# W_down and W_up laid out with neighbouring rows in a partition, in a persistent adapter kernel

## The reference

```
h = einsum('bsh,bhk->bsk', x, W_down[role]) + b_down[role]      # 1024 -> 512
h = gelu(h)                                                     # exact gelu
u = einsum('bsk,bkh->bsh', h, W_up[role]) + b_up[role]          # 512 -> 1024
y = x + u
out = layernorm(y) * gamma[role] + beta[role]
```

## Time and profile before

| | us |
|---|---|
| median of 3 runs | 1418.1 (1417.81 to 1418.21) |
| the profiled execution, its time | 1418.03 |
| its span | 1416.3 |
| TensorE busy in the span | 1401.5 |
| VectorE busy | 1207.1 |
| ScalarE busy | 778.0 |
| GpSimd busy | 200.9 |

### The profile page before, as it was taken

One profiled execution on the slowest core, in us unless ns is written; L12 is line 12 of the kernel. 1 busy time (PEld: TensorE's weight loads), 2 busy tenths in 40 slices (PEclk: granted clock), 3 DMA queues, 4 the chain that ended last, 5 costly groups with the idle time before them and its releaser, 6 DMA issues.

```text
span 1416.3 us, 29328 instructions
## 1 busy us (share of the span) xinstructions
PE 1401.5 (99%) x6175; PEld 1158.7 (82%) x6176; DVE 1207.1 (85%) x1456; ACT 778.0 (55%) x2053; POOL 200.9 (14%) x300
## 2 busy tenths in 40 slices
PE   8999999999999999999999999999999999999997
PEld 6888888888888888888888888888888888888886
DVE  7799988888888888888888899988888888888887
ACT  5555555555555555555555555555555555555555
POOL 3377311100000000000000377311100000000000
PEclk9999999999999999999999999999999999999999
DMA  9678777766666656666666778767766666666664
GB/s 228 184 227 236 210 218 199 212 195 200 184 194 198 194 183 196 198 193 185 194 199 192 215 227 230 225 199 211 207 197 185 200 199 186 185 195 201 189 186 149
DMA packets 208868, 283.49 MB, mean 200 GB/s; under 512 B 25791, under 2 KB 155584, under 8 KB 208846
## 3 DMA queue, kind: packets, MB, share of 16 engines
q1 hardware_dynamic: 201870, 269.60, 62.3%
q0 software_dynamic: 5888, 12.07, 5.0%
q10 hardware_dynamic: 1088, 1.57, 0.4%
HBM read 183.27 MB, written 99.88 MB: 200 GB/s over the span
## 4 chain that ended last, share of the span: by engine, by line
PE 97%; DVE 1%; DMA 1%; ACT 0%; issue 0%; DVEq 0%; ACTq 0%
PE p_down L1077 16%; PE p_up L1079 16%; PE p_down L1079 16%; PE p_up L1077 16%; PE p_down L1078 16%; PE p_up L1078 16%; DMA row<-in_L_cond_W_down 0%; DMA x_quad<-in_x 0%; DVE row L997 0%; PE p_hT L1073 0%; DMA w_raw<-in_itok_B 0%; DVE row L794 0%; DVE wd_lo L732 0%; DVE row L840 0%; ACT wd_hi L548 0%
## 5 line engine op out<-in xcount | busy, mean ns | idle before, releaser
L1077 PE MATMUL p_down<-wd_hi,xT_hi 128*128 x1012 | 393.9, 389 | 1.1 <-DVE wd_lo L732 0.6
L1079 PE MATMUL p_down<-wd_hi,xT_lo 128*128 x1012 | 393.7, 389 | 0.0
L1078 PE MATMUL p_down<-wd_lo,xT_hi 128*128 x1012 | 393.7, 389 | 0.0
L1077 PE MATMUL p_up<-wu_hi,hT_hi 128*128 x1008 | 392.3, 389 | 0.0
L1079 PE MATMUL p_up<-wu_hi,hT_lo 128*128 x1008 | 392.1, 389 | 0.0
L1078 PE MATMUL p_up<-wu_lo,hT_hi 128*128 x1008 | 392.1, 389 | 0.0
L585 ACT ACTIVATE hT_hi<-p_hT 128x512 fp32r<-128x512 f32 x126 | 75.5, 599 | 382.0 <-DVE p_hT L774 379.8
L794 DVE SCALAR_TENSOR_TENSOR row<-p_up,row 128x1024 f32<-128x1024 f32 x126 | 154.1, 1223 | 125.5 <-PE p_up L1079 125.5
L571 ACT ACTIVATE xT_hi<-xT_raw 128x1024 fp32r<-128x1024 f32 x125 | 132.7, 1062 | 187.7 <-PE p_down L1079 185.5
L1077 PEld LDWEIGHTS p_down<-wd_hi,xT_hi 128*128 128x128 f32 x1012 | 189.9, 188 | 40.8 <-issue 1.8
L1079 PEld LDWEIGHTS p_down<-wd_hi,xT_lo 128*128 128x128 f32 x1012 | 190.2, 188 | 39.6
(11 more groups left out here) (174 smaller groups left out, 982.8 us busy)
## 6 DMA issues: line engine op xcount, KB each, us to landing
x_quad<-in_x SPq DMA_DIRECT2D x510, 128.0 KB, 3.5
row<-in_x SPq DMA_DIRECT2D x126, 512.0 KB, 4.1
out<-row SPq DMA_DIRECT2D x126, 512.0 KB, 2.7
h_dram<-h SPq DMA_DIRECT2D x125, 256.0 KB, 4.1
h_quad<-h_dram SPq DMA_DIRECT2D x500, 64.0 KB, 2.0
w_raw<-in_L_cond_W_down POOLq DMA_DIRECT2D x64, 64.0 KB, 3.2
w_raw<-in_L_cond_W_up POOLq DMA_DIRECT2D x64, 64.0 KB, 3.8
row<-in_L_cond_W_up SPq DMA_DIRECT2D x16, 128.0 KB, 4.2
```

The source lines that it names most:

```text
L1077: pe.matmul(dst, a_hi, w_hi, start=first, stop=False)
L1078: pe.matmul(dst, a_hi, w_lo, start=False, stop=False)
L1079: return pe.matmul(dst, a_lo, w_hi, start=False, stop=last)
```

## The change

Partition p now holds rows 8p to 8p+7 of W_down (chunk c is row 8p+c) and rows 4p to 4p+3 of W_up. A piece of the first role is then contiguous in HBM for a partition (two rows of W_down, 4 KB) or a single row of W_up, and comes by one transfer over 128 partitions in place of four. To turn x so that it fits, VectorE's transposes read `x_quad` with a step of 8 floats (chunk c takes the features 8a+c of a block of 256) and `h_quad` with a step of 4. The bias add of the first three items writes h with a step of 128 floats in its innermost dimension. At the start, ScalarE issues pieces 0 and 1 whole before its table load, rounds piece 0 before it issues its half of x, and no longer takes part in piece 2.

```diff
-        wd_view = W_down.rearrange("r (q c a) k -> r q a c k", q=NQ, a=BLK)
-        wu_view = W_up.rearrange("r (q c a) h -> r q a c h", q=NQ, a=BLK)
+        wd_view = W_down.rearrange("r (p c) k -> r p c k", c=HC)
+        wu_view = W_up.rearrange("r (p c) h -> r p c h", c=KC)
...
-        def load_first(eng, n, quads=range(NQ)):
+        def load_first(eng, n):
             buf = row[n % RING]
-            for q in quads:
-                if n < FD:
-                    w = FC // K
-                    dst = buf[BLK * q:BLK * q + BLK, 0:FC].rearrange("p (c k) -> p c k", c=w)
-                    eng.dma_start(dst, wd_view[R - 1, q, :, n * w:n * w + w, :]).then_inc(first_raw[n], 16)
-                else:
-                    eng.dma_start(buf[BLK * q:BLK * q + BLK, 0:FC], wu_view[R - 1, q, :, n - FD, :]).then_inc(
-                        first_raw[n], 16)
+            if n < FD:
+                w = FC // K
+                eng.dma_start(buf[:, 0:FC].rearrange("p (c k) -> p c k", c=w), wd_view[R - 1, :, n * w:n * w + w, :]).then_inc(
+                    first_raw[n], 16)
+            else:
+                eng.dma_start(buf[:, 0:FC], wu_view[R - 1, :, n - FD, :]).then_inc(first_raw[n], 16)
...
-            load_first(sp, FD - 2, range(NQ // 2, NQ))
+            load_first(sp, FD - 2)
             load_first(sp, FD - 1)
...
-                            src = wd_view[bass.ds(r, 1), q, :, bass.ds(2 * m + par, 1), :].rearrange("o a c k -> (o a) (c k)")
+                            src = wd_view[bass.ds(r, 1), BLK * q:BLK * q + BLK, bass.ds(2 * m + par, 1), :].rearrange(
+                                "o a c k -> (o a) (c k)")
...
-            load_first(act, 0, range(0, 1))
+            load_first(act, 0)
+            load_first(act, 1)
             act.wait_ge(out_ready, 1)
             act.activation(factor[:, 0:1], opener[:, 2:3], ACT.Gelu)
-            load_first(act, 0, range(1, NQ))
-            load_first(act, 1)
+            round_first(0)
             act.wait_ge(first_known, 1)
             load_quads(act, act.value_load(first_numbers[0:1, 0:1], min_val=0, max_val=B - 1), 0, range(NQ // 2, NQ))
...
-            round_first(0)
             act.wait_ge(order_in_psum, 1)
...
             round_half(0, 0)
-            load_first(act, FD - 2, range(0, NQ // 2))
...
             def turn_x(raw, par, c):
                 return (raw.rearrange("p c (g t) -> p g c t", g=NQ),
-                        x_quad[par][:, :, c * BLK:c * BLK + raw.shape[1] * BLK].rearrange("p g (c a) -> p g c a", a=BLK))
+                        x_quad[par][:, :, :].rearrange("p g (a c) -> p g c a", c=HC)[:, :, c:c + raw.shape[1], :])
...
                 dve.transpose(p_hT[:, :].rearrange("p (c g t) -> p g c t", c=KC, g=NQ),
-                              h_quad[:, :, :].rearrange("p g (c a) -> p g c a", a=BLK)).then_inc(h_transposed, 1)
+                              h_quad[:, :, :].rearrange("p g (a c) -> p g c a", c=KC)).then_inc(h_transposed, 1)
...
-                    by_chunk = dict(q=NQ, c=KC, a=BLK)
-                    dve.tensor_tensor(h[:, :].rearrange("p (c q a) -> p q c a", **by_chunk),
-                                      src.rearrange("p (q c a) -> p q c a", **by_chunk),
-                                      bias.rearrange("p (q c a) -> p q c a", **by_chunk), ALU.add).then_inc(biased, 1)
+                    dve.tensor_tensor(h[:, :].rearrange("p (c j) -> p j c", c=KC),
+                                      src.rearrange("p (j c) -> p j c", c=KC),
+                                      bias.rearrange("p (j c) -> p j c", c=KC), ALU.add).then_inc(biased, 1)
```

More of the change, by code:

```diff
@@ L456, in load_params @@
                     pool.wait_ge(loaded, 16 * part + 16)
-            raw_once = 16 * NQ
-            pool.wait_ge(first_raw[FD + FU - 1], raw_once)
+            pool.wait_ge(first_raw[FD + FU - 1], 16)
             pool.wait_ge(numbers_ready, 1)
@@ L507, in _ @@
                         for q in range(NQ):
-                            src = wu_view[bass.ds(r, 1), q, :, bass.ds(m, 1), PC * par:PC * par + PC].rearrange(
+                            src = wu_view[bass.ds(r, 1), BLK * q:BLK * q + BLK, bass.ds(m, 1), PC * par:PC * par + PC].rearrange(
                                 "o a c h -> (o a) (c h)")
@@ L526, in first_piece, with round_first @@
             buf = row[n % RING][:, 0:FC]
-            count = 16 * NQ
             if n < FD:
-                return buf, wd_hi[:, n * FC:n * FC + FC], wd_lo[:, n * FC:n * FC + FC], count
+                return buf, wd_hi[:, n * FC:n * FC + FC], wd_lo[:, n * FC:n * FC + FC]
             m = n - FD
-            return buf, wu_hi[:, m * FC:m * FC + FC], wu_lo[:, m * FC:m * FC + FC], count
+            return buf, wu_hi[:, m * FC:m * FC + FC], wu_lo[:, m * FC:m * FC + FC]
         @block.scalar
         def _(act):
-            load_first(act, 0, range(0, 1))
+            load_first(act, 0)
+            load_first(act, 1)
             act.wait_ge(out_ready, 1)
             act.activation(factor[:, 0:1], opener[:, 2:3], ACT.Gelu)
-            load_first(act, 0, range(1, NQ))
-            load_first(act, 1)
+            def round_first(n):
+                buf, hi, lo = first_piece(n)
+                act.wait_ge(first_raw[n], 16)
+                act.activation(hi, buf, ACT.Copy).then_inc(first_hi, 1)
+            round_first(0)
             act.wait_ge(first_known, 1)
             load_quads(act, act.value_load(first_numbers[0:1, 0:1], min_val=0, max_val=B - 1), 0, range(NQ // 2, NQ))
[L545 to L548, removed]
             def copy_param(n, src, at, size, loaded):
@@ L729, in split_first @@
             def split_first(n):
-                buf, hi, lo, _ = first_piece(n)
+                buf, hi, lo = first_piece(n)
                 dve.wait_ge(first_hi, n + 1)
```

## The result

The changed kernel takes 1464.3 us (median of 6 runs, 1459.8 to 1468.0) against 1418.1 us: 1.032 times the kernel before, 95% interval 1.031 to 1.034. It is slower by 46 us. The profile is of an execution of 1463.15 us with a span of 1461.4.

The account below looks back on a forecast made before the run. TensorE's matmuls were taken to set the time, VectorE next in line. From 1418.03 us, 0.76 came off for the hole at the start and 0 was added for everything else: 1417.3 us, range 1415.8 to 1490.

Parts of the forecast that it names:

- The price of the steps: VectorE's transposes of x and h with stepped reads: between 0 and 1.08 ns more an element, taken as 0.
- The slack: VectorE's path over both transposes to h's low part, before TensorE's up product: 1.03 us an item, covering up to 0.67 ns an element.
- first rival: Stepped transposes cost VectorE a second interval, 0.98 ns an element: item 11.37 us against 10.88, 1478 to 1490 us; chance 0.19.
- GpSimd's stretches: Where GpSimd splits weights and VectorE has no idle time: at 0.4 ns, about 20 items pay 0.61 us, at most +12.
- The first bias adds: L811 in the first three items, writing with a step of 128 floats: nothing up to 0.55 us each, taken as 0.
- The start: TensorE's waits for first transfers: piece 2 of W_down issued whole by SyncE lands earlier, -0.76 us, or 0 at the other end.
- third rival: At the start, transfers only change places and nothing is gained: 1418.0, or 1419.4 us with piece 0's slowest landing; chance 0.20.
- The hole ahead of item 0's second half product: TensorE's wait at 17.78 to 18.54 for piece 2 of W_down, 0.76 us, forecast to close.
- Item 0's x: ScalarE's transfers of x, issued behind piece 0's rounding: 0 late by the likely landing, up to 1.4 us by the slowest.
- The weight loads of GpSimd and the single transfers: Later roles' loads beside a gapless TensorE: 0; SyncE's 16 fewer issues save 7.4 us of queue time, worth nothing by itself.
- The slower side: Chance of a measurably slower kernel, 0.26: 0.19 for a full second interval on stepped reads plus 0.07 for a smaller price.
- the partial price: Stepped transposes on VectorE cost 0.67 to 0.98 ns an element (1459 us at 0.83), or less (at most 1430 at 0.4); chance 0.09.

## Why the prediction was wrong

- **The price of the steps** is the step that failed. "I take nothing: the nearest row is L811" was wrong: L811's runs of 32 floats don't touch what a step of 4 or 8 does. The price was 0.90 and 0.72 ns an element in the loop, about 0.7 for the transposes alone at steps 4 and 8. That lies between the prediction's ends of 0 and 1.08 ns and over the 0.67 ns from which it had the loop break. In these runs a read that takes two floats of 16 neighbouring bytes (step 2) is free, and one that takes a single float of them costs the same at steps 4, 8 and 16 within 0.12 us. This agrees with the rule of the Trainium skill that the prediction weighed (page "Advanced Engine Details and Errata", section SBUF Cachelines: lines of 16 bytes, at least two accesses to each for full speed). It doesn't prove the 16 bytes: any limit on the distance between 8 and 16 bytes would give the same times, and step 3, which could tell, wasn't run. The other page, "VectorE: DVE Perf Modes" in its section on Mode 1×, says that strides work in this mode. Every stepped instruction here did work, and was slower; that the sum would stay as it is was the prediction's own step from that sentence.
- **The slack** of 1.03 us on the path of h's low part was right, as a mechanism and in size. x's 0.92 us alone left the quiet stretches at 10.88 us, both together (1.29 us) broke them. From VectorE's end to the waiting matmul it is 0.14 to 0.24 us in the steady items. The first rival's own sum with the measured price, 3.88 + 1.29 + 0.24 + 5.64 + 0.10 = 11.15 us, is the measured mean of the steady items. So its 11.37 was off by the price alone (1.29 in place of 1.51 us).
- **GpSimd's stretches** were seen ("felt only where VectorE has no idle time"), with the full price for about 20 items as the most. That holds as an upper end: 0.92 us for 20 items is 18, measured 13; 0.37 us is 7, measured 2. What was missing is a feedback. Seven items in a row (the two rows below are the first L790 and the eighth) take 86.31 us, 12.33 each, which is 1.45 more than 10.88 and not 1.29. VectorE's three plain instructions there stand beside GpSimd's item after item, its x addition L780 at 1.73 us, x's low part L764 at 1.63 and the scaling L813 at 2.31, together 5.67; in the kernel before the same three vary from 3.7 to 5.5 us. In the profiled execution of the changed kernel the second of GpSimd's stretches, 800 to 1000 us, loses 27 matmuls, in that of the kernel with stepped reads alone 43. That is 3.6 us, and the two executions are 3.5 us apart. So how many items are long differs between the two.

```profile
71.26 1.23 DVE L790 SCALAR_TENSOR_TENSOR row<-p_up,row 128x1024 f32<-128x1024 f32 x1 [0.16 <-PE p_up L1074]
...
157.57 1.21 DVE L790 SCALAR_TENSOR_TENSOR row<-p_up,row 128x1024 f32<-128x1024 f32 x1
```

- **The first bias adds** (nothing up to 0.55 us each) took 1.07 to 1.12 us in place of 0.68 to 0.69. With plain transposes around them the last matmul came no later than before, so covering them with other work was right there. In the changed kernel, whose start is late anyway, it wasn't: TensorE waits 0.39 us for item 0's h (last matmul before at 25.00, the next at 25.62).
- **The start**: as the third rival had it, there is no gain (the holes change places). The hole ahead of item 0's second half product closes in the kernels that have the new order at the start and no steps of 4 or 8. In the changed kernel it is still there, smaller (19.00 to 19.64, 0.41 us lost), with the same subtraction of piece 2 as releaser, and a larger one stands ahead of item 1's (15.39 to 16.36). The terms that failed are two. Item 0's x, taken as 0 late: ScalarE issues it from 6.06, not 5.62, with the rounding of piece 0 starting at 5.13 and not near 4.6. And the price of the steps once more: a half transpose takes 1.11 to 1.21 us there in place of 0.67 to 0.71, and nothing covers it. Of the 0.56 us by which TensorE's first product is late (12.75, before 12.19) x's later landing makes 0.17 and the longer transpose about 0.40. These rows show it in the changed kernel:

```profile
5.13 1.06 ACT L542 ACTIVATE wd_hi<-row 128x1024 fp32r<-128x1024 f32 x1 [1.86 <-DMA row<-in_L_cond_W_down]
...
6.06 0.90 ACTq L275 DMA_DIRECT2D x_quad<-in_x  x2
...
9.98 1.11 DVE L744 STREAM_TRANSPOSE xT_raw<-x_quad 128x512 f32<-128x512 f32 x1 [0.45 <-DMA x_quad<-in_x]
...
12.75 0.49 PE L1072 MATMUL p_down<-wd_hi,xT_hi 128*128 x1 [0.37 <-issue]
...
16.36 0.49 PE L1072 MATMUL p_up<-wd_hi,hT_hi 128*128 x1 [0.59 <-issue]
...
19.64 0.49 PE L1072 MATMUL p_down<-wd_hi,xT_hi 128*128 x1 [0.26 <-DVE wd_lo L728]
```

- **The weight loads of GpSimd and the single transfers** at nothing: right, by the run without stepped reads.
- **The chances.** The slower side was right with 0.26 and stood within the range; the partial price, the case that it was, had 0.09. That rival's sum at the measured 0.84 ns, 1.29 - 1.03 + 0.10 = 0.36 us for each of 124 items, gives 1463 us, near the 1464.3 measured, and this is partly luck: it charges all items alike, where the steady ones lose 0.27 us and seven of them 1.45. A rule that speaks against a change and one row that only resembles it should not have been weighed at nearly three to one for the row.

## What to carry to other kernels

Before a layout moves a stride onto the critical engine, price the step by a single instruction at that step: for float32 on VectorE a step of 2 was free and steps of 4, 8 and 16 cost about 50 to 60% of a plain instruction's time by itself (77% for x's transpose in the loop), for a transpose, an addition and a multiplication alike, and for the multiplication's writes as for its reads. Then compare it with the slack of the one path that the next engine waits for, not with the engine's idle time in all: two prices that cost little one by one (13 and 2 us) cost 49 together, and another order of the same instructions took back most of it. A gain of a microsecond in the start has to be followed to the last matmul, because closing one hole there mostly opened another.

## What was not expected of the hardware

The price of a step was not a full second interval: 1.98 us for 1024 floats in place of 1.25, and at step 16 it was a little less than at steps 4 and 8 (1.89 against 1.98 and 2.00), for the transposes and in the same way for the multiplication (1.03 against 1.07 and 1.09) and the addition. In GpSimd's stretches the instructions of both VectorE and GpSimd were longer, with a rhythm: in the changed kernel GpSimd's subtraction of 512 floats took 2.06 to 2.21 us (1.3 at its shortest in the kernel before) and VectorE's scaling of 1024 floats 2.31 us (1.28 in quiet stretches) in both items read between 104 and 130 us. That GpSimd's work is what lengthens VectorE's is seen from the quiet stretches; the other direction is read from the two standing side by side, as no stretch has GpSimd splitting without VectorE.
